# Token loop of a graph-convolution kernel: layer-1 results in other PSUM banks, a low part moved from VectorE to GpSimd, one halving instead of two

## The reference, cut to what matters

```python
def _layer(x, A, W, b, g, be, m, v, relu):
    x = jnp.einsum('btvc,co->btvo', x, W)
    x = jnp.einsum('uv,btvo->btuo', A, x)
    x = (x + b - m) * (g * jax.lax.rsqrt(v + EPS)) + be
    return jax.nn.relu(x) if relu else x
# 3 -> 128 -> 128 -> 64 channels
return x.mean(axis=2)
```

## Time and profile before

| | us |
|---|---|
| median of 3 runs (1706.45 to 1708.33) | 1706.89 |
| the profiled execution | 1707.45 |
| its span, first to last instruction | 1705.5 |
| token loop (start some 70, end some 1215 us into the span) | some 1145 |
| busy in the span: PE / DVE / POOL / ACT | 1586.6 / 1409.0 / 1344.2 / 1167.0 |

### The profile page before, as it was taken

The page is one execution under the profiler, slowest core; times in us unless marked ns, Lnnn a source line. Parts: engine busy times, 40 slices in busy tenths (PEclk is TensorE's granted clock), DMA queues, the critical chain, the costliest instruction groups (busy, mean ns, idle before and its releaser), DMA issues. The chain is left out here.

```text
span 1705.5 us, 65032 instructions
## 1 busy us (share of the span) xinstructions
PE 1586.6 (93%) x22590; PEld 1130.4 (66%) x22621; DVE 1409.0 (83%) x3355; ACT 1167.0 (68%) x2706; POOL 1344.2 (79%) x1496
## 2 busy tenths in 40 slices
PE   8599999999999999999999999999776899999999
PEld 8466666666666666666666666666565588888887
DVE  7388888888888888888888888888766799999998
ACT  3477777777777777777777777777243487887886
POOL 2388888888888888888888888888444688888887
PEclk9999999999999999999999999999788799999999
DMA  5200000000000000000000000000001000000001
GB/s 118 83 7 6 7 7 6 7 7 6 7 7 6 7 7 6 7 7 6 7 7 6 7 7 6 7 7 6 19 21 53 1 0 0 0 0 0 0 0 37
DMA packets 21666, 21.62 MB, mean 13 GB/s; under 512 B 12254, under 2 KB 19342, under 8 KB 21271
## 3 DMA queue, kind: packets, MB, share of 16 engines
q1 hardware_dynamic: 18554, 19.07, 4.1%
q0 software_dynamic: 1120, 1.44, 0.3%
q10 hardware_dynamic: 1972, 0.86, 0.2%
HBM read 14.43 MB, written 6.92 MB: 13 GB/s over the span
## 5 line engine op out<-in xcount | busy, mean ns | idle before, releaser
L693 DVE SCALAR_TENSOR_TENSOR y<-ps,negb,abar 128x375 f32<-128x375 f32 x820 | 477.7, 603 | 129.3 <-PE ps L595 124.8
L649 POOL TENSOR_TENSOR y0lo<-y_whole,y0hi 128x384 f16<-128x384 f32 x410 | 374.6, 914 | 144.9 <-ACT y_whole L625 132.0
L580 PE MATMUL ps<-AThi,y0hi 64*128 64x150 f16 (+1 forms) x4920 | 435.6, 217 | 5.7 <-POOL y0lo L649 3.6
L580 PE MATMUL ps<-AThi,y0lo 64*128 64x150 f16 (+1 forms) x4920 | 436.3, 215 | 0.0
L580 PE MATMUL ps<-ATlo,y0hi 64*128 64x150 f16 (+1 forms) x4920 | 436.0, 215 | 0.0
L624 ACT ACTIVATE y0hi<-ps 128x384 f16<-128x384 f32 x410 | 201.0, 490 | 328.8 <-PE ps L563 324.9
L658 POOL TENSOR_TENSOR y<-y 128x370 f32<-128x370 f32 x410 | 398.4, 972 | 7.6 <-DVE y L693 1.8
L1239 POOL TENSOR_TENSOR rs<-var,expo 128x8 f32<-128x8 f32 x180 | 313.0, 1749 | 66.0 <-DVE var L1307 66.0
L599 PE MATMUL ps<-z_whole,W1s 128*128 128x375 f32 x820 | 340.7, 497 | 0.1
L682 DVE SCALAR_TENSOR_TENSOR y0lo<-ps,y0hi 128x384 f16<-128x384 f32 x410 | 226.5, 552 | 73.8 <-ACT y0hi L626 73.8
L580 PEld LDWEIGHTS ps<-AThi,y0hi 64*128 64x128 f16 x4920 | 256.9, 94 | 21.0 <-issue 11.2
(11 more groups left out here) (197 smaller groups left out, 2421.0 us busy)
## 6 DMA issues: line engine op xcount, KB each, us to landing
z_static<-z_rows SPq DMA_DIRECT2D x410, 18.0 KB
xs<-in_x_v SPq DMA_DIRECT2D x5, 720.7 KB, 9.4
z_rows<-zp SPq DMA_DIRECT2D x10, 240.0 KB
h_rows<-h SPq DMA_DIRECT2D x16, 96.0 KB, 1.8
h2r<-h_rows SPq DMA_DIRECT2D x6, 256.0 KB, 2.7
out<-h2r SPq DMA_DIRECT2D x6, 256.0 KB, 2.3
z_rows<-zp POOLq DMA_DIRECT2D x5, 240.0 KB, 3.3
h<-in_txt SPq DMA_DIRECT2D x1, 512.0 KB, 4.9
```

Source lines behind the costliest of these rows:

```text
L580: last = nc.tensor.matmul(ps[:, Z1B + 2 * p + j, f0 * V:f0 * V + w], y[rows, par, p, t * C:(t + 1) * C], a[rows, BAND0[t]:BAND0[t] + w], s ...
L649: nc.gpsimd.tensor_tensor(y0lo[:, par, p, 0:HC], y0f[:, p, :], y0hi[:, par, p, 0:HC], ALU.subtract).then_inc(y0lo_by_pool, 1)
L693: nc.vector.scalar_tensor_tensor(y1[:, par, 2 * p + i].rearrange("p f v -> p (f v)"), ps[:, Y1B + i, 0:GV], negb1[:, 0:1], abar[:].rearran ...
```

## The change

- y0_whole gets a third slot. For pair 0 ScalarE writes the relu of bank 1 to it as well (a fourth relu), and GpSimd makes both low parts of pair 0. Pair 1 stays as it was: one low part on GpSimd, one on VectorE.
- The pairs of layer 0 swap places: pair 0 comes first in a group, pair 1 after the mixes. Pair 0's layer 0 waits for VectorE's low part of pair 1 of the group before; pair 1's waits for ScalarE's two whole parts of pair 0.
- Layer 1 of pair 0 goes to banks 5 and 4 (those of pair 1's mix), that of pair 1 stays in 6 and 7. The waits follow.
- ScalarE's order: `y0_high` pair 0, `z1_high` pair 0, `z1_high` pair 1, `y0_high` pair 1.
- GpSimd halves once, and VectorE sums 38 nodes (U1 to V) in place of 19. `weigh` gets a wait for an old sum.
- VectorE's body is in a new order.

```diff
-        y0f = sb("y0_whole", [P, PAIRS, HC])
+        y0f = sb("y0_whole", [P, PAIRS + 1, HC])
-        Y0B, Z1B, Y1B = 0, 2, 6
+        Y0B, Z1B = 0, 2
+        Y1B = ((5, 4), (6, 7))
...
                 def layer0(it, par, p, loads):
-                    n = y0_unit(it, p)
-                    if late(n, 1):
-                        pe.wait_ge(y0f_done, n)
-                        pe.wait_ge(y0lo_by_dve, n)
+                    if p == 1:
+                        pe.wait_ge(y0f_done, it * 3 + 2)
+                    elif late(it, 1):
+                        pe.wait_ge(y0f_done, it * 3)
+                        pe.wait_ge(y0lo_by_dve, it)
...
                 def mix(it, par, p):
-                    n = pair_unit(it, p)
-                    pe.wait_ge(y0lo_by_pool, y0_unit(it, p) + 1)
-                    pe.wait_ge(y0lo_by_dve, y0_unit(it, p) + 1)
-                    if late(n, 2):
-                        pe.wait_ge(z1lo_done, n - 1)
-                        pe.wait_ge(z1f_done, n - 1)
+                    n = unit(it, p)
+                    pe.wait_ge(y0lo_by_pool, it * 3 + 2 + p)
+                    if p == 1:
+                        pe.wait_ge(y0lo_by_dve, it + 1)
+                    if late(it, 1):
+                        if p == 0:
+                            pe.wait_ge(z1lo_done, n - 1)
+                            pe.wait_ge(z1f_done, n - 1)
+                        else:
+                            for i in range(2):
+                                pe.wait_ge(y1_done[i], unit(it - 1, 0) + 1)
...
                 def layer1(it, par, p):
...
-                    if late(n, 1):
-                        pe.wait_ge(y1_done[0], n)
-                    o = ps[:, Y1B, 0:GV]
+                    if p == 0:
+                        pe.wait_ge(z1f_done, unit(it, 1) + 1)
+                    elif late(it, 1):
+                        pe.wait_ge(y1_done[0], n - 1)
+                    o = ps[:, Y1B[p][0], 0:GV]
...
                     pe.wait_ge(z1f_done, n + 1)
-                    if late(n, 1):
-                        pe.wait_ge(y1_done[1], n)
+                    if p == 0:
+                        pe.wait_ge(z1lo_done, unit(it, 1) + 1)
+                    elif late(it, 1):
+                        pe.wait_ge(y1_done[1], n - 1)
...
                 def body(it, par, pair, last=False):      # TensorE
                     if not last:
-                        layer0(it + 1, 1 - par, 1, pair + 2)
+                        layer0(it + 1, 1 - par, 0, pair + 2)
                     mix(it, par, 0)
                     mix(it, par, 1)
                     if not last:
-                        layer0(it + 1, 1 - par, 0, pair + 2)
+                        layer0(it + 1, 1 - par, 1, pair + 2)
                     if late(it, 1):
                         layer1(it - 1, 1 - par, 1)
                     layer1(it, par, 0)
...
                     nc.scalar.activation(y0hi[:, par, p, HC:2 * HC], ps[:, Y0B + 1, 0:HC], ACT.Relu).then_inc(y0hi_done, 1)
+                    if p == 0:
+                        nc.scalar.activation(y0f[:, 2, :], ps[:, Y0B + 1, 0:HC], ACT.Relu).then_inc(y0f_done, 1)
...
                 def body(it, par, pair, last=False):      # ScalarE
                     if not last:
+                        y0_high(it + 1, 1 - par, 0)
+                    z1_high(it, par, 0)
+                    z1_high(it, par, 1)
+                    if not last:
                         y0_high(it + 1, 1 - par, 1)
-                    z1_high(it, par, 0)
-                    if not last:
-                        y0_high(it + 1, 1 - par, 0)
-                    z1_high(it, par, 1)
...
                     nc.gpsimd.tensor_tensor(y[:, :, U1:2 * U1], y[:, :, U1:2 * U1], y[:, :, 0:U1], ALU.add).then_inc(halved, 1)
-                    pool.wait_ge(halved, n + 1)
-                    nc.gpsimd.tensor_tensor(y[:, :, U2:V], y[:, :, U2:V], y[:, :, U1:U2], ALU.add).then_inc(quartered, 1)
...
                 def weigh(it, par, p, i):
+                    if late(it, 2):
+                        dve.wait_ge(pooled, it - 1)
...
-                    nc.vector.tensor_reduce(pooledT[:, :, bass.ds(it * GF, GF)], y1[:, par, :, :, U2:V], AX_X,
+                    nc.vector.tensor_reduce(pooledT[:, :, bass.ds(it * GF, GF)], y1[:, par, :, :, U1:V], AX_X,
...
                 def body(it, par, pair, last=False):      # VectorE
-                    if late(it, 1):
-                        weigh(it - 1, 1 - par, 0, 1)
+                    z1_low(it, par, 0)
                     if late(it, 2):
                         pool_nodes(it - 2, par)
-                    if not last:
-                        y0_low(it + 1, 1 - par, 1)
-                    z1_low(it, par, 0)
+                    z1_low(it, par, 1)
                     if late(it, 1):
                         weigh(it - 1, 1 - par, 1, 0)
                         weigh(it - 1, 1 - par, 1, 1)
+                    weigh(it, par, 0, 0)
                     if not last:
-                        y0_low(it + 1, 1 - par, 0)
-                    z1_low(it, par, 1)
-                    weigh(it, par, 0, 0)
+                        y0_low(it + 1, 1 - par, 1)
+                    weigh(it, par, 0, 1)
```

More of the change, by code:

```diff
@@ L506, in tokenise @@
         halved = sem("halved")
-        quartered = sem("quartered")
         pooled = sem("pooled")
-        Y0B, Z1B, Y1B = 0, 2, 6
+        Y0B, Z1B = 0, 2
+        Y1B = ((5, 4), (6, 7))
         LAST = GROUPS - 1
-        U1, U2 = V // 2, V // 2 + (V - V // 2) // 2
+        U1 = V // 2
         def steps(eng, body):
@@ L526, in late, with unit @@
             return not isinstance(n, int) or n >= k
-        def y0_unit(it, p):
-            return it * PAIRS + 1 - p
-        def pair_unit(it, p):
+        def unit(it, p):
             return it * PAIRS + p
@@ L596, in layer1 @@
                     pe.wait_ge(z1f_done, n + 1)
-                    if late(n, 1):
-                        pe.wait_ge(y1_done[1], n)
-                    nc.tensor.matmul(ps[:, Y1B + 1, 0:GV], W1s[:], z1f[:, par, p, :], start=True, stop=True).then_inc(y1_ready[1], 1)
+                    if p == 0:
+                        pe.wait_ge(z1lo_done, unit(it, 1) + 1)
+                    elif late(it, 1):
+                        pe.wait_ge(y1_done[1], n - 1)
+                    nc.tensor.matmul(ps[:, Y1B[p][1], 0:GV], W1s[:], z1f[:, par, p, :], start=True, stop=True).then_inc(y1_ready[1], 1)
+                layer0(0, 0, 0, 1)
                 layer0(0, 0, 1, 1)
-                layer0(0, 0, 0, 1)
                 def body(it, par, pair, last=False):
                     if not last:
-                        layer0(it + 1, 1 - par, 1, pair + 2)
+                        layer0(it + 1, 1 - par, 0, pair + 2)
                     mix(it, par, 0)
@@ L620, in y0_high @@
                 def y0_high(it, par, p):
-                    act.wait_ge(y0_ready, y0_unit(it, p) + 1)
+                    act.wait_ge(y0_ready, unit(it, p) + 1)
                     if late(it, 1):
-                        act.wait_ge(y0lo_by_pool, y0_unit(it, p) - 1)
+                        act.wait_ge(y0lo_by_pool, it * 3 - 1 + p)
                     nc.scalar.activation(y0hi[:, par, p, 0:HC], ps[:, Y0B, 0:HC], ACT.Relu).then_inc(y0hi_done, 1)
@@ L626, in y0_high @@
                     nc.scalar.activation(y0hi[:, par, p, HC:2 * HC], ps[:, Y0B + 1, 0:HC], ACT.Relu).then_inc(y0hi_done, 1)
+                    if p == 0:
+                        nc.scalar.activation(y0f[:, 2, :], ps[:, Y0B + 1, 0:HC], ACT.Relu).then_inc(y0f_done, 1)
                 def z1_high(it, par, p):
-                    act.wait_ge(z1_ready, pair_unit(it, p) + 1)
+                    act.wait_ge(z1_ready, unit(it, p) + 1)
                     nc.scalar.activation(z1hi[:, par, p, :], ps[:, Z1B + 2 * p, 0:GV], ACT.Identity).then_inc(z1hi_done, 1)
                     nc.scalar.activation(z1f[:, par, p, :], ps[:, Z1B + 2 * p + 1, 0:GV], ACT.Identity).then_inc(z1f_done, 1)
+                y0_high(0, 0, 0)
                 y0_high(0, 0, 1)
-                y0_high(0, 0, 0)
                 def body(it, par, pair, last=False):
                     if not last:
+                        y0_high(it + 1, 1 - par, 0)
+                    z1_high(it, par, 0)
+                    z1_high(it, par, 1)
+                    if not last:
                         y0_high(it + 1, 1 - par, 1)
-                    z1_high(it, par, 0)
-                    if not last:
-                        y0_high(it + 1, 1 - par, 0)
-                    z1_high(it, par, 1)
                 steps(act, body)
@@ L647, in y0_low @@
                 def y0_low(it, par, p):
-                    pool.wait_ge(y0f_done, y0_unit(it, p) + 1)
+                    pool.wait_ge(y0f_done, it * 3 + 1 + 2 * p)
                     nc.gpsimd.tensor_tensor(y0lo[:, par, p, 0:HC], y0f[:, p, :], y0hi[:, par, p, 0:HC],
                                             ALU.subtract).then_inc(y0lo_by_pool, 1)
```

(31 more changed lines are left out.)

4 lines of the change are left out of this document (1 added, 3 removed).

## The result

The changed kernel took 1909.55 us (median of 4 runs, 1905.97 to 1911.44) against 1707.61 for the one before, run beside it: 1.118 times, 95% interval 1.1161 to 1.1199. The forecast was 1902, range 1878 to 1936.

What follows compares the result with a forecast made beforehand. A cycle of waits through nearly all of VectorE's body bounds the changed kernel: 6.52 us against 5.556, +0.96 over 202 laps is 194 us, plus 1, on 1707.45 gives 1902.5 (1902 against the median); range 1878 to 1936.

Steps and rivals of the forecast that it cites:

- The old lap: Kernel before: cycle of weighing, layer 1, layer 0, relus and low part, twice over VectorE, once over ScalarE, 5.56 us.
- The new lap: Changed kernel: from layer 0 over ScalarE's relus and z1hi through VectorE's body to its low part, 6.52 us; chance 0.85.
- The allowance at TensorE's wait: Layer 0 of pair 0 starts 0.10 us after VectorE's low part, plus 0.05 us for uncertain wait latencies.
- The reduce: VectorE's sum over 128x760 in place of 128x380 takes 0.943 us; the next instruction starts after 0.86 us.
- The fourth relu: ScalarE's added relu for pair 0 costs 0.37 us and stands ahead of z1hi of pair 0 in its queue.
- (a) The banks: Layer 1 of pair 0 in banks 5 and 4: the wait for the weighing goes, shortening the former cycle; no size given.
- the sum: Whole kernel: 202 laps of 0.96 us more, 194 us, plus 1 us for first and last groups, added to 1707.45.
- Idle times: Per group, VectorE idles some 2 us before z1_low, ScalarE some 1.8 before its first relu, TensorE about 1 before layer 0.
- the clock's rival: TensorE's idle microsecond per group lowers its clock: 2630 us throughout, 1975 with one lap in ten; chance 0.06.
- One reading of the prediction: At 67.12, layer 0's six matmuls took 0.51 us against 0.34 in the loop, read as a 1.2 GHz clock.
- TensorE as the bound: Freed banks let groups follow at TensorE's own 5.06 us, making the kernel faster, 1607 us; chance 0.03.
- GpSimd had idle time: GpSimd needs 4.69 us a group against 4.75 before, so it shows idle time; otherwise the prediction is wrong.

Runs made afterwards that it cites:

- the first experiment: The changed kernel with only VectorE's reduce moved to the end of its body: 1798.5 us, ratio 1.0527 to the kernel before.

## Why the prediction was right, point by point

- *The old lap*, ring of weighing, layer 1, layer 0, relus and low part: borne out by the reordering of TensorE alone, which hid the weighing and gave 3.7%.
- *The new lap*: 6.52 us forecast, 6.555 measured. The allowance at TensorE's wait was the term most off: 0.10 + 0.05 forecast, 0.11 and 0.24 in turn, 0.175 in the mean, which is 0.025 of the 0.035. The profiled executions lie 202 us apart, 7 more than the 195 forecast: the last reduce starts 198.9 us later (1413.9 in place of 1215.0), and the other 2.9 us arose behind it, in stages that the change does not touch. The forecast had put nothing there.
- *The reduce*: 0.943 us forecast, 0.934 measured; its step 0.86, measured 0.85 (807.31 to 808.16).
- *The fourth relu*: 0.37 us ahead of z1hi, so forecast. Taking it out with GpSimd's third low part gave 66 us back.
- *(a) The banks*: I wrote that this alone would shorten the old lap. Wrong: it costs 190 us there. The paragraph did name the wait that takes the place of the old one, for pair 1's z1_whole and z1lo, but did not walk it in the old order, where it is over later than the weighing. In the sum I had given the banks nothing, and in the new order that was right: of the new waits only the 0.2 us at L605 is left, and it is not in the ring.
- *Idle times*: VectorE's some 2 us and TensorE's 1 us were 2.10 to 2.24 and 1.10 to 1.24. ScalarE's was put at 1.8 and is 2.19 to 2.33, and VectorE's busy time fell by 0.29 us a group (4.65 to 4.36), not by 0.07; the sum uses neither.
- *What I did not see*: in the reduce's place ScalarE would have made VectorE wait 0.30 us anyway. It did not touch the sum; it made the first experiment miss.
- *The rivals*: the granted clock stayed at 1.00 through the loop although TensorE idled 1.1 to 1.24 us a group, so the clock's rival fell. The Trainium skill ("TensorE: Matmul & The Clock Gate", "A second HAM failure mode: psum-queue depth-cycling") reports of another kernel that short idles between groups that cycle banks make the clock swing; this trace does not agree, at 1.00 with these idles. One run did show the clock fall, at the start of its loop: with the banks alone TensorE had idled 2.20 us before 77.50, the granted clock was 0.50 from 78.7 to 82.0, and in its later laps, with 0.97 us idle, 1.00 again. One reading of the prediction is open: it took the 0.51 us at 67.12 for the lower level, but the granted clock of that stretch is 1.00 (67.10 to 67.70); the same six matmuls also took 0.50 us in the banks-alone kernel at 78.70, where it was 0.50. TensorE as the bound is reached only when the lap is cleared (1645 us in the kernel before, reordered, and 1622 with the change's banks; I gave that rival 1607). GpSimd had idle time, as forecast: busy for 210.6 of 300 us, 4.59 a group against 4.69.

Not tried: the fourth relu without GpSimd's third low part, and the new waits of the weighings on an old reduce by themselves.

## What to carry to other kernels

Where no engine is full, write down the ring of waits and walk it once more for the new order, with everything that stands in each queue ahead of the instruction that closes it; busy time told nothing here, since the change lowered it on VectorE and cost 12%. A short instruction in front of the one that another engine waits for costs its step in each lap, less the idle time that would stand there without it (0.30 of 0.855 us here). A few places later it can be nearly free, or cost again if it brings a wait of its own: the reduce last in the body waited for GpSimd and cost 75 us. A buffer shared with another pair removes one wait and adds another: ask which of the two is over sooner in the present order.

## What the runs showed of the hardware that I had not expected

The delay from VectorE's low part to the layer 0 that waits for it alternated between 0.11 and 0.24 us, in bodies that differ only in their place in the loop; with the low parts as before it was 0.10 and 0.24 in turn. ScalarE's relus had lengths of 0.49 to 0.60 us (804.79 and 808.48 above), while the starts in the run stayed 0.36 to 0.39 apart: the length grew along an unbroken run of instructions, the rate did not.
